# A graph-attention layer on one core: adj stored in the order of its loads, stores behind all loads, last pieces over three pairs

## The reference

```python
def gat(node_features, adjacency_matrix, W, b_W, a_vec, b_a):
    h = node_features @ W.T + b_W
    a1, a2 = a_vec[:128], a_vec[128:]
    e = (h @ a1)[:, None] + (h @ a2)[None, :] + b_a[0]
    e = jnp.where(e > 0, e, 0.2 * e)
    scores = jnp.where(adjacency_matrix > 0, e, -9e15)
    return jax.nn.softmax(scores, axis=1) @ h

h = jnp.maximum(_layernorm(x, axis=-1), 0.0)
return x + gat(h, adj, W, b_W, a_vec, b_a)
```

## Time and profile before

| | us |
|---|---|
| median of 3 runs | 208.16 (207.99 to 208.33) |
| the profiled execution, its own time | 207.64 |
| its span in the trace | 206.1 |
| PE, DVE, ACT busy in the span | 198.3, 183.7, 142.3 |

### The profile page before, as it was taken

One profiled execution on the slowest core, in us unless ns is written; L12 is line 12 of the kernel. 1 busy time (PEld: TensorE's weight loads), 2 busy tenths in 40 slices (PEclk: granted clock), 3 DMA queues, 4 the chain that ended last, 5 costly groups with the idle time before them and its releaser, 6 DMA issues.

```text
span 206.1 us, 7172 instructions
## 1 busy us (share of the span) xinstructions
PE 198.3 (96%) x3183; PEld 192.1 (93%) x3183; DVE 183.7 (89%) x271; ACT 142.3 (69%) x129; POOL 43.5 (21%) x60
## 2 busy tenths in 40 slices
PE   7969999999999999999999999999999999999794
PEld 7648878999999999999999999999999999999694
DVE  4779889999999699987999999979999998979954
ACT  2679777798771777689777775797577767897000
POOL 1002479599995010420000000000000000000000
PEclk9999999999999999999999999999999999999999
DMA  5999999999999999999999999999999999992312
GB/s 180 364 411 405 400 410 406 406 409 406 408 432 398 406 410 409 405 409 409 405 409 411 400 387 417 409 408 407 409 406 408 359 413 414 408 405 118 99 47 64
DMA packets 24160, 75.66 MB, mean 367 GB/s; under 512 B 1600, under 2 KB 5952, under 8 KB 24000
## 3 DMA queue, kind: packets, MB, share of 16 engines
q1 hardware_dynamic: 23984, 75.06, 92.7%
q10 hardware_dynamic: 144, 0.13, 0.3%
HBM read 73.08 MB, written 2.11 MB: 365 GB/s over the span
## 4 chain that ended last, share of the span: by engine, by line
DMA 63%; ACT 14%; PE 6%; issue 6%; DVE 5%; SPq 4%; DVEq 0%
DMA adj_sb<-in_adj_t 63%; ACT mask L379 10%; DVE w L459 4%; ACT xT L394 3%; SPq L268 2%; PE ps L834 2%; PE ps L836 2%; PE ps L840 2%; SPq L273 2%; PE ps L808 1%; SPq L284 1%; DVE xT L497 1%; ACT H L342 1%; PE ps L798 0%; ACT hT L337 0%
## 5 line engine op out<-in xcount | busy, mean ns | idle before, releaser
L834 PE MATMUL ps<-V,w 128*128 128x129 f16 x1024 | 177.3, 219 | 1.2 <-DVE w L459 1.2
L836 PE MATMUL ps<-V,w 128*128 128x129 f16 x1024 | 177.3, 223 | 0.0
L840 PE MATMUL ps<-V,w 128*128 128x129 f16 x1024 | 177.3, 218 | 0.0
L379 ACT ACTIVATE mask<-adj_sb 128x2048 bf16<-128x2048 int32 x63 | 119.9, 1915 | 39.1 <-DMA adj_sb<-in_adj_t 38.9
L459 DVE SCALAR_TENSOR_TENSOR w<-g_row,pairs,mask 128x1024 f32<-128x1024 f32 x96 | 117.7, 1282 | 9.5 <-ACT mask L379 8.5
L834 PEld LDWEIGHTS ps<-V,w 128*128 128x128 f16 x1024 | 99.2, 97 | 3.0 <-DVE w L459 1.6
L840 PEld LDWEIGHTS ps<-V,w 128*128 128x128 f16 x1024 | 102.0, 100 | 0.0
L836 PEld LDWEIGHTS ps<-V,w 128*128 128x128 f16 x1024 | 99.8, 97 | 1.0 <-issue 1.0
L459 DVE SCALAR_TENSOR_TENSOR w<-ps,pairs,mask 128x1024 f32<-128x1024 f32 x31 | 37.6, 1271 | 1.3 <-ACT mask L379 1.3
L788 POOL PARTITION_ALL_REDUCE bad<-bad x1 | 0.4, 380 | 114.6 <-DVE bad L532 114.6
L746 POOL TENSOR_TENSOR x_sb<-x_sb,b_row 128x512 f32<-128x512 f32 x8 | 10.0, 1304 | 0.0
(11 more groups left out here) (93 smaller groups left out, 62.4 us busy)
## 6 DMA issues: line engine op xcount, KB each, us to landing
adj_sb<-in_adj_t SPq DMA_DIRECT2D x64, 1024.0 KB, 11.2
xT<-in_x_t SPq DMA_DIRECT2D x8, 256.0 KB, 7.9
x_sb<-in_x_p SPq DMA_DIRECT2D x3, 512.0 KB, 11.3
g_row<-g_dram SPq DMA_DIRECT2D x1, 1536.0 KB, 10.6
out<-xT SPq DMA_DIRECT2D x3, 512.0 KB, 11.5
x_sb<-in_x_p SPq DMA_DIRECT2D x2, 256.0 KB, 4.5
out<-xT SPq DMA_DIRECT2D x1, 192.0 KB, 2.1
out<-xT SPq DMA_DIRECT2D x3, 64.0 KB, 1.5
```

The source lines that it names most:

```text
L379: nc.scalar.activation(mask[:, m % MASKS, :], adj_sb[:, m % HELD, :], ACT.Relu, scale=CONNECTED).then_inc(mask_ready, 1)
L834: nc.tensor.matmul(sums[:, bank, a, :], w16[:, m % SLOTS, col:col + P, 1], V[:, jt, 0:NF], start=(jt == 0 and a == 0), stop=False, skip_gr ...
L836: nc.tensor.matmul(sums[:, bank, a, :], w16[:, m % SLOTS, col:col + P, 1], V[:, jt, NF:2 * NF], start=False, stop=False, skip_group_check= ...
L840: last = nc.tensor.matmul(sums[:, bank, a, :], w16[:, m % SLOTS, col:col + P, 0], V[:, jt, 0:NF], start=False, stop=(jt == NT - 1), skip_g ...
```

## The change

Four things change.

1. The host stores the transposed adj in the order of its loads: block m holds the 1 MiB of pair m, and in it each partition's two runs of 1024 int32 lie side by side. A load then reads 128 contiguous pieces of 8 KB in place of 256 pieces of 4 KB, and the whole block is contiguous in memory. Bytes, destination and order of the loads are as before.
2. The stores of groups 0 and 1 leave the loop over the loads and stand behind all of them.
3. `ENDS` is 3: the pieces go over pairs 61 to 63, and pair 60 is worked through whole.
4. A constant `_GROUP` names the eight tiles of a group for the kernel and the host.

```diff
-    ENDS = 4
+    ENDS = 3
...
                 def load_adj(m):
...
-                    sp.dma_start(adj_sb[:, m % HELD, :].rearrange("p (a n) -> p a n", a=2),
-                                 adjt_v[:, 2 * at:2 * at + 2, group * GC:(group + 1) * GC]
-                                 ).then_inc(adj_loaded[m % HELD], 16)
+                    sp.dma_start(adj_sb[:, m % HELD, :], adj_t[m, :, :]).then_inc(adj_loaded[m % HELD], 16)
...
-                    if group >= 2 and at == STORE_AT:
-                        store(group - 2, GI * (group - 2), GI * (group - 1))
-                store(NG - 2, GI * (NG - 2), GI * (NG - 1))
+                for r in range(NG - 1):
+                    store(r, GI * r, GI * (r + 1))
...
-    arrays["in_adj_t"] = np.ascontiguousarray(np.asarray(inputs["adj"]).T)
+    adj = np.asarray(inputs["adj"])
+    pairs = adj.shape[0] // (2 * P)
+    arrays["in_adj_t"] = np.ascontiguousarray(
+        adj.T.reshape(pairs, 2, P, -1, _GROUP * P).transpose(3, 0, 2, 1, 4).reshape(-1, P, 2 * _GROUP * P))
```

More of the change, by code:

```diff
@@ L41 @@
 _SETS = ((0, 4), (4, 8), (8, 16), (16, 24), (24, 32))
+_GROUP = 8
 def gat_layer_kernel(nc, x_p, x_t, adj, adj_t, w_pack, b_W, out):
@@ L57, in gat_layer_kernel @@
     NCH = NT // CT
-    GI = 8
+    GI = _GROUP
     GC = GI * P
@@ L77, in gat_layer_kernel @@
     REST_AT = HELD + MASKS
-    STORE_AT = 6
     SETS = _SETS
@@ L248, in gat_layer_kernel @@
         adj_v = adj.rearrange("(g p) n -> p g n", p=P)
-        adjt_v = adj_t.rearrange("(g p) n -> p g n", p=P)
         out_v = out.rearrange("(g p) d -> p g d", p=P)
@@ L275, in load_adj @@
                 def load_adj(m):
-                    group, at = divmod(m, PAIRS)
                     if m >= HELD:
```

## The result

The changed kernel takes **205.61 us**, the median of 6 runs (205.25 to 206.54). The kernel before, on the same chip beside it, takes 208.07. The ratio is 0.9877, 95% interval 0.9837 to 0.9917: 2.5 us, or 1.2%, faster. A ratio here compares the fast runs of both kernels, so it isn't exactly the quotient of the two medians. The forecast had 206.7 us and a range from 206.0 to 207.6. The profiled execution of after took 206.0 us with a span of 204.4 (before: 207.64).

The account below looks back on a forecast made before the run. PE was taken to bound the long middle, with gains possible only at start and end. Terms -1.53 (stall) + 0.35 (tail) - 0.25 (start) = -1.43 us took the median 208.16 to 206.7 us, range 206.0 to 207.6.

Parts of the forecast that it names:

- the stall: PE's two waits for pair 63's weights, 0.86 + 0.67 = 1.53 us, which `ENDS = 3` would remove.
- the start: Before pair 4, the 8 KB adj pieces land pair 3's load earlier, so PE gains 0.25 us.
- PE is the bound of the long middle: From 36 to 193 us PE needs 2.76 us a pair, the loads 2.57, so PE sets the pace.
- a faster stream of loads is worth nothing there: In the middle, ready weights in four slots cover upstream waits; faster loads can help only before 36 or after 193 us.
- both are in time, the second by 0.24 us: With three pairs PE wants pair 63's halves at 195.22 and 195.74; they came at 194.30 and 195.50.
- The tail, +0.35: Behind PE's end, shorter pieces (1.035 us) no longer cover DVE's 1.41 us row of work and checks: 0.35 us back.
- Just covered now: Before the change, DVE's 1.41 us of last checks run beside 1.38 us of PE, ending up 0.03 us behind it.
- The rate, 418 GB/s: Adj loads in 8 KB pieces run at 418 GB/s in place of 408, 2.5% faster, bounds 0% and 3.4%.
- between 0 and 0.35: Bounds on the 0.25 us start gain, from the 0% and 3.4% bounds of the load rate.
- the start gains more: Rival: the slowest DMA engine finishes pair 0's load half a microsecond earlier, giving 206.2 us; chance 0.11.
- The stores, nothing: Moving two stores of 1.4 us each behind all loads costs nothing, covered by idle DMA slices; uncovered, 2.8 us.
- this doesn't shorten the sum: Without the stores pair 63 comes up to 1.4 us earlier, which only widens the 0.24 us margin.

Follow-up runs that it names:

- run d: A further profile of the unchanged kernel before: pair 4 starts at 34.90, gaps at pairs 62 and 63 2.59 us, time less the gaps 205.54 us.
- g: A further profile of the unchanged kernel before in which PE's clock rose late: pair 4 starts at 35.98, gaps 0.99 us; it took 207.57 us.
- run h: A further profile of the unchanged kernel before, at mean clock 0.992: pair 4 starts at 34.86, gaps 2.59 us; such executions took 209.08 us or more.
- theory G: Changed kernel with `ENDS = 4` plus two idle DVE additions ahead of pair 63's weights, testing whether PE's wait there brings clock 0.992: median 207.11 us.
- G2: Changed kernel with `ENDS = 4` plus three idle DVE additions ahead of pair 62's weights, testing whether gaps at two close pairs bring clock 0.992: 207.63 us.
- run b: A further profile of the unchanged kernel before: pair 4 starts at 35.39, gaps at pairs 62 and 63 2.95 us; it took 209.01 us.

## Why the prediction was right and wrong

**Two terms mis-sized, and one given to the wrong edit.** The sum had the stall at 1.53 us and the start at 0.25; they measure 2.07 and 0.63, and that is what took the time out of the range. And the stall was credited to `ENDS = 3` alone. The runs show that the new loads remove it by themselves, and that within the whole `ENDS = 3` only costs. The paragraphs below take the steps one by one.

**PE as the bound: wrong at one point.** "PE is the bound of the long middle" holds for the middle. But the step "a faster stream of loads is worth nothing there" doesn't follow. The stock of weights covers the middle, and the end asks for more: with pieces over four pairs PE wants pair 63 after 3 x 18 matmuls of pairs 60 to 62 in place of 3 x 48, so 90 x 0.0575 = 5.2 us before its turn. The rows for it were shown: DVE waits 1.38 us for a mask at pair 59 and has no slack from there to pair 63. What makes that mask earlier makes the end earlier. The forecast used this for a margin of 0.24 us and not for the end.

**The stall, 1.53 us: right in place, mis-sized.** The waits at pair 63 went. They measure 2.07 us in the mean of eight profiles, since the gap is the difference of two times which both move from run to run. The forecast read it from one execution that was 0.52 us faster than the median, and carried these 0.52 us over to the new kernel unchanged. In the main they were stall too: 2.07 is 0.54 us more than 1.53. The step "both are in time, the second by 0.24 us" didn't hold either when `ENDS = 3` was tried alone: 0.50 us of wait was left.

**The tail, +0.35: right.** 0.34 in the pair of profiles, 0.33 in the other (0.56 against 0.23), 0.37 in pooled medians. Its reason was right in the difference: 18 matmuls of PE cover 0.35 us less of the checks than 24. The level was misread. "Just covered now" and "0.03" leave out that DVE begins the row at 201.82 only 0.19 us after PE has ended the piece (24 matmuls ahead of its last slot's end at 203.01), so the last check stood 0.22 us behind PE before and stands 0.56 behind it after, not 0.375.

**The rate, 418 GB/s: right**, 419 measured. The DMA row of 80 to 110 us, after and then the kernel with the new loads alone, against 408 in the earlier trace rows:

```profile
DMA packets 1723, 12.58 MB, mean 419 GB/s; under 512 B 191, under 2 KB 191, under 8 KB 191
DMA packets 1719, 12.58 MB, mean 419 GB/s; under 512 B 188, under 2 KB 188, under 8 KB 188
```

The pieces are half as many and the stream 2.7% faster. The rule of the Trainium skill ("DMA: Bandwidth & Descriptors", section "Why small descriptors are slow (HBM only)") gave 1.2% as an estimate. The measurement decides here: the longer piece saves more than twice what that rule counts, or the new place of the data gives the rest. No run parts the two.

**The start, -0.25: right in sign, too small.** In the profiles whose clock rose early pair 4 begins at 35.07 in the mean with 4 KB pieces (eight profiles) and at 34.44 with 8 KB (five): 0.63 us. Pair 3's load lands at 26.5 against 25.9. The step that failed is the bound "between 0 and 0.35", made of the mean rate. The rival "the start gains more" was the nearer one. That a load is complete with its slowest engine, on which that rival rests, fits these numbers; no run isolates it. SP also issues this load earlier, at 8.8 to 9.6 us in place of 10.0 to 10.5. What makes up the 0.4 us beyond the rate stays open.

**The stores, nothing: right as a term, for the wrong reason.** Their move alone gained 2.4 us, because they lay in the stream that sets the end; "this doesn't shorten the sum" was no general truth. But with the new loads nothing is left to gain: the new loads alone take 205.06 us, and after with `ENDS = 4`, which is the new loads and the moved stores, takes 205.21 over its 12 runs.

**The sum.** With the stall 2.07, the start 0.63 and the tail 0.35 the change is -2.07 - 0.63 + 0.35 = -2.35 us, against -2.46 measured. The terms aren't that sure: with the stall of the executions whose clock rose early, 2.35, the sum is -2.6. In the terms of the stream, the change takes the end from pair 63's weights back to PE.

**What beats the changed kernel.** After with `ENDS = 4` (205.2) and the new loads alone (205.06) are the fastest. Between these two the runs don't decide.

## What to carry to other kernels

A consumer with stock hides a producer that falls behind, until the stock is gone; so a stream isn't free because its consumer doesn't wait in the middle, and the last items tell which of them sets the end. Where several edits attack one wait, time each alone before you add them up: here 1.5, 3.2 and 2.4 us made 2.5. Then take each out of the whole, too: one edit was only cost. A wait that is the difference of two moving times should be read from several executions.

## What the runs showed of the hardware

**PE begins at the lower clock in every execution, and when the clock rises differs.** PE's first work in after and in its second profile; L844 are 16 matmuls that only warm PE up:

```profile
1.22 3.78 PE L844 MATMUL ps<-ones 128*128 128x128 f32 x16 [1.22 <-POOL ones L711]
5.67 1.11 PE L792 MATMUL ps<-xT,centre 128*128 128x512 f32 x2
7.69 2.07 PE L802 MATMUL ps<-wp,hT 128*128 128x130 f32 x16
...
5.69 2.05 PE L792 MATMUL ps<-xT,centre 128*128 128x512 f32 x2
9.67 2.53 PE L802 MATMUL ps<-wp,hT 128*128 128x130 f32 x16
```

The matmuls of L844 start 0.21 us apart; those of L802, which are no smaller (130 columns, 128 in L844), start 0.11 apart once the clock is up. All twenty profiles begin like that. So PE begins at 1.2 GHz and later runs at 2.4. The row of the granted clock says 1.00 for the start all the same: the trace's first record of the clock comes only with the rise (5.68 us in after, 10.87 in its second profile), and the view counts the time before it as full. By these first records the clock rises at 4.1 to 6.8 us in twelve profiles and at 9.7 to 10.9 in six; two profiles (d and g) have no record, and their matmuls show an early and a late rise. In between PE works without a pause. The two matmuls of L792 take 1.11 us behind the rise, 2.05 ahead of it, and 1.72 in the profile of after with `ENDS = 4`, where the clock rises between them. What decides when it rises isn't known.

With the late rise pair 4 begins at 36.29 in place of 34.18 to 34.43. In the kernel before this costs little, for PE waits at the end anyway (0.99 and 1.46 us there, against 2.35 in the mean of the others): such executions took 207.57 and 208.31, the others with a full clock at the end 207.34 to 209.01. In after it shows: 207.19 against 205.08 and 206.0. So the new kernel is now open to what PE's start does. The profiles of both kernels with `pack(2)` moved and of both with additions on DVE have the late rise too.

**The clock can fall at the very end.** In 30 of 99 executions of the kernel before with a mean clock on record, it was 0.992, and these took 209.08 us or more; the others, but for three (209.20, 210.06 and one of 711.91), took less. One of them is run h. Its windows, with the columns of the earlier trace rows, and below them run d over the last of these stretches but one:

```profile
194.00:196.00 2.00, 0.69 (x9) 0.52 (x9) 2.00 (x2) 0.00 (x0) 0.00 (x0) 1.00 0.69 206
196.00:198.00 2.00, 1.94 (x21) 1.94 (x22) 0.92 (x6) 0.00 (x0) 0.00 (x0) 0.59 0.19 56
198.00:200.00 2.00, 2.00 (x23) 2.00 (x22) 0.39 (x2) 0.00 (x0) 0.00 (x0) 0.56 0.32 92
200.00:202.00 2.00, 2.00 (x39) 2.00 (x37) 0.81 (x5) 0.00 (x0) 0.00 (x0) 1.00 0.02 6
...
198.00:200.00 2.00, 2.00 (x39) 2.00 (x37) 0.56 (x4) 0.00 (x0) 0.00 (x0) 1.00 0.33 98
```

After the gaps PE runs at 1.2 GHz in place of 2.4 for 3.4 us, from 196.34 to 199.75: 21 to 23 matmuls in 2 us where d has 34 to 39. (The trace of d has no record of the clock, so its 1.00 says nothing; its 39 matmuls do.) The gaps of h and d are the same, 2.59 us, and the last check comes 1.61 us later in h. None of the 29 executions of after and of it with `ENDS = 4` had this, and none of the 23 with a single edit. With the stall put back at pair 63 it came in 0 of 12, at pair 62 in 1 of 12 (209.1 us). So the fall came only in kernels with gaps at pairs 62 and 63, but what decides whether it comes stays open: the 12 runs of theory G were on a chip where the kernel before had it in 1 of 18, so their 0 says little, one case in 12 doesn't settle G2, and run b had the larger gaps, 2.95 us, without it.

**A small operation of DVE can last as long as POOL's operation beside it.** The two operations L574 and L577 of `pack(2)` took 0.62 and 0.55 us in their old place and 0.97 and 0.98 behind pair 7. POOL in after and in after with `pack(2)` moved:

```profile
40.67 0.62 POOL L755 TENSOR_TENSOR V<-H,evr 128x258 f16<-128x258 f32 x1 [2.95 <-DVE evr L584]
41.25 0.62 POOL L756 TENSOR_TENSOR prod<-H,evr 128x258 f32<-128x258 f32 x1
...
45.12 1.05 POOL L755 TENSOR_TENSOR V<-H,evr 128x516 f16<-128x516 f32 x1
46.12 1.05 POOL L756 TENSOR_TENSOR prod<-H,evr 128x516 f32<-128x516 f32 x1
```

In after POOL's operations end at 41.30 and 41.87, and DVE's at 41.33 and 41.91; with `pack(2)` moved POOL's end at 46.17 and 47.17, and DVE's at 46.20 and 47.21. So each of DVE's ends 0.03 to 0.04 us behind the one of POOL, and it takes longer in the new place, where POOL's operations are twice as wide. Earlier in the kernel, where POOL is idle, the same two lines take 0.17 and 0.18 us for half as many elements. No run changes POOL's work alone, so this is read from the times only.
